# Attention beside an FP4 gated layer: GpSimd out of the gate chain, a finer grid for the pieces, and TensorE's blocks on either side of the values

## The chip, the cores and the metric

The kernel runs on one core of a Trainium2 chip. The metric is the device time in microseconds (us) of one execution: 2633.95 us in the median of 3 runs, 2632.21 to 2635.04. The engines are TensorE (PE; its weight loads are listed as PEld), VectorE (DVE), ScalarE (ACT), GpSimd (POOL) and SyncE (SP, which only issues transfers here).

## The reference

For x of shape (4, 2048, 256) and xn, its layer norm without weights, the result is

```
out = x + attention(xn) + ffn(xn)
attention: q, k, v = split(xn @ Wqkv.T); 16 heads of 16; causal softmax(q k / 4) v; @ Wout.T + bout
ffn:       gate = q4(xn) @ q4(w_gate).T ; up = q4(xn) @ q4(w_up).T      (704 columns)
           h = silu(gate) * up ; y = q4(h) @ q4(w_down).T
q4: blocks of 16 along the last dimension, scale = max|.| / 6, values rounded to the FP4 grid, times scale
```

All is float32.

## The kernel before

Four stages follow one another: the weights, the projections to q, k and v, the largest score of every row (the shift), and the stage that matters here, `main_phase`. It begins shortly before 1000 us and lasts to the end.

In `main_phase` attention and the gated layer run beside each other. Attention is a list of 640 steps. There are 4 batches of 4 groups of 4 heads (`NHG`); a group has 4 chunks of 512 queries, and chunk c has 4(c+1) steps, one for each block of 128 keys at or below the diagonal. So a group has 40 steps. The last four steps of a chunk touch the diagonal and are 512, 384, 256 and 128 queries wide (`Step.width`); all others are 512. In step n TensorE computes the scores of two halves (L1031, and L1037 for the mask) into `S[0]` and `S[1]`, ScalarE makes `probs` of them (L1180, one exp for each half), and TensorE multiplies the probabilities of step n-1 with v into `O` (`values`, L1052). A half of `S` is free for the next scores when its exp is done. When a chunk is over, VectorE turns `O` (L1409, L1410), and only then may the first values of the next chunk write it (semaphore `o_free`); it goes on with sums, reciprocals and scaling (L1414 to L1428; the last, L1428, in every other group). This is `normalise`, and VectorE does it behind all its pieces of that step.

The gated layer handles 64 tiles of 128 tokens, 16 to a batch, 4 to a group of steps. Its work is cut in pieces, and each piece has a place, a mark k out of `MARKS` per tile. `place_marks` spreads the marks of a batch's 16 tiles evenly over the batch's steps, where a step counts as its width plus `STEP_COST`; a mark in the first half of a step is `early`, else `late`. Each engine walks the same list of steps in its own program order, and waits on semaphores where data cross: ScalarE does exp 0, early pieces, exp 1, late pieces; VectorE and GpSimd early, late; TensorE scores, early and late pieces, values of the step before.

The pieces of tile t in order of data, with TensorE's blocks in capitals: X_TURN (L1066) of the quantised x into `F[0]`; ScalarE's `xt_hi` (L1185) and VectorE's `xt_lo` (L1363); GATE for two chunks of 352 columns into `F[0]` and `F[1]`, 6 matmuls each (L1073); VectorE's copy to `gate_sb` (L1368), which frees the bank for UP; GpSimd's `below` = min(gate, 0) (L1255) beside ScalarE's tanh(gate/2) (L1189); ScalarE's `decay` = exp(below) (L1193); GpSimd's gate x decay (L1259); on VectorE the sign bit cleared (L1372), `silu` = (|tanh| + 1) x that (L1376) and `gated` = 0.5 x up x silu (L1380). VectorE then makes the block scales of h (L1331 to L1337), GpSimd normalises (L1244), VectorE rounds (L1341 to L1347), GpSimd scales back (L1250). H_TURN of tile t-1 (L1099) turns it into `F[0]` and `F[1]`, ScalarE makes `ht_hi` (L1198), VectorE `ht_lo` (L1396), and DOWN multiplies in two halves of 9 matmuls into `F[1]` (L1110); VectorE adds it to y (L1402). The same scales, normalising and rounding are done for x, one tile ahead. In half of the tiles two blocks PROJECT (L1119) bring finished attention rows through `Wout`, and VectorE adds them (L1433). SyncE loads x two tiles ahead and stores y at mark 0.

## Time and profile before

| | |
|---|---|
| median of 3 runs | 2633.95 us (2632.21 to 2635.04) |
| profiled execution | 2634.47 us, span 2632.8 us |
| busy, share of the span | PE 2336.7 us (89%), DVE 1962.6 (75%), ACT 1956.8 (74%), POOL 918.4 (35%) |
| mean granted clock of TensorE | 0.975 of full |

The span goes from the first to the last instruction. In the profile a group of instructions has its source line, engine, output and input names without buffer numbers; "idle before" is the time that an engine stood still ahead of an instruction, with what released it. Waits are put down to the last thing that came. Durations overlap on TensorE, as its matmuls are pipelined, so for the length of a block the chain of waits is the better view.

### The profile page before, as it was taken

How to read it: one execution, taken by the hardware profiler on the slowest of the kernel's cores; microseconds unless marked ns; L12 is line 12 of the kernel's file. 1: busy time of each engine (PE TensorE's matmuls, PEld its weight loads, DVE VectorE, ACT ScalarE, POOL GpSimd, SP SyncE). 2: the span in 40 equal slices, each digit the busy share in tenths (PEclk: the TensorE clock that was granted, in tenths of full speed). 3: DMA queues.
4: the chain of work that ended last, by engine and by line, in shares of the span. 5: the costliest groups of instructions: out<-in, count | busy, mean ns of one | idle time of the engine just before them, and what ended most of it. 6: DMA issues, size and time to landing. Idle time of an engine off the chain costs nothing.

```text
span 2632.8 us, 86210 instructions
## 1 busy us (share of the span) xinstructions
PE 2336.7 (89%) x34104; PEld 1294.7 (49%) x34104; DVE 1962.6 (75%) x5676; ACT 1956.8 (74%) x3342; POOL 918.4 (35%) x780
## 2 busy tenths in 40 slices
PE   2896999999999957999999989899998999989998
PEld 1784444444444424445455545455544455554455
DVE  6675999999999975766666667576676666667665
ACT  1343999999999956787777777777777777777775
POOL 3212233333333323333333333333333433334332
PEclk7898999999999988999999999999999999999999
DMA  2576445555555513101201101201011021011000
GB/s 62 176 225 146 69 72 73 73 72 72 73 72 73 72 28 75 28 12 33 61 19 42 38 17 30 60 23 36 22 39 28 13 66 40 19 38 30 13 20 30
DMA packets 94537, 143.82 MB, mean 55 GB/s; under 512 B 24896, under 2 KB 73920, under 8 KB 93632
## 3 DMA queue, kind: packets, MB, share of 16 engines
q1 hardware_dynamic: 89792, 129.50, 25.3%
q0 software_dynamic: 4352, 8.92, 1.4%
q8 instruction: 266, 4.36, 0.7%
q14 instruction: 127, 1.04, 0.2%
HBM read 104.20 MB, written 34.14 MB: 53 GB/s over the span
## 4 chain that ended last, share of the span: by engine, by line
PE 35%; DVE 11%; ACT 10%; issue 7%; DMA 0%; SPq 0%; POOL 0%; DVEq 0%; ACTq 0%; POOLq 0%
PE O L1052 10%; ACT probs L1180 8%; PE F L1073 7%; PE S L1031 6%; PE F L1110 6%; PE F L1119 2%; DVE silu L1376 2%; DVE o_turned L1409 1%; PE S L1037 1%; DVE o_packed L1421 1%; PE F L1099 1%; ACT ht_hi L1198 1%; DVE gated L1380 1%; DVE o_turned L1410 1%; DVE h_amax L1331 1%
## 5 line engine op out<-in xcount | busy, mean ns | idle before, releaser
L1180 ACT ACTIVATE probs<-S 128x1024 f32<-128x1024 f32 (+3 forms) x1280 | 1081.7, 899 | 381.2 <-PE S L1031 195.1
L775 ACT ACTIVATE m_excess<-m_DIFF 128x512 f32<-128x512 f32 (+7 forms) x1536 | 646.8, 472 | 85.0 <-PE m_DIFF L735 39.8
L793 DVE CUSTOM_DVE_ANT_0 m_excess<-m_S,m_excess 128x512 f32<-128x512 f32 (+7 forms) x1536 | 700.5, 530 | 11.1 <-PE m_S L735 9.4
L1052 PE MATMUL O<-probs,v_sb 64*32 64x512 f32 (+3 forms) x10240 | 615.9, 536 | 18.5 <-DVE o_turned L1410 15.8
L1031 PE MATMUL S<-q_st,k_st 64*32 64x512 f16 (+3 forms) x10240 | 440.7, 349 | 141.9 <-ACT probs L1180 99.9
L733 PE MATMUL m_S<-m_k,m_q 128*128 128x512 f16 (+7 forms) x1536 | 482.1, 324 | 26.7 <-DVE m_row_max L793 17.4
L733 PE MATMUL m_DIFF<-m_k,m_q_diff 128*128 128x512 f16 (+7 forms) x1536 | 476.9, 318 | 26.4 <-DMA m_q_diff<-s_q 26.1
L1031 PEld LDWEIGHTS S<-q_st,k_st 64*32 64x32 f16 x10240 | 170.3, 91 | 521.4 <-ACT probs L1180 356.0
L677 POOL TENSOR_TENSOR m_q_diff<-m_zero,m_q 48x4096 f16<-48x4096 f16 x32 | 224.4, 7011 | 428.0 <-DMA m_q<-s_q 417.3
L733 PEld LDWEIGHTS m_S<-m_k,m_q 128*128 128x128 f16 x1536 | 148.0, 96 | 276.7 <-DVE m_row_max L793 195.9
L735 PE MATMUL m_S<-m_future,m_ident 128*128 128x64 bf16 x1024 | 197.0, 193 | 0.0
L735 PE MATMUL m_DIFF<-m_future,m_ident 128*128 128x64 bf16 x1024 | 196.5, 193 | 0.0
L1052 PEld LDWEIGHTS O<-probs,v_sb 64*32 64x32 f32 x10240 | 131.6, 105 | 122.6 <-ACT probs L1180 53.5
L733 PEld LDWEIGHTS m_DIFF<-m_k,m_q_diff 128*128 128x128 f16 x1536 | 150.5, 98 | 69.5 <-issue 27.1
L1376 DVE SCALAR_TENSOR_TENSOR silu<-tanh,gate_sb 128x352 f32<-128x352 f32 x128 | 103.5, 809 | 107.3 <-POOL gate_sb L1259 104.0
L1255 POOL TENSOR_SCALAR below<-gate_sb 128x352 f32<-128x352 f32 x128 | 139.4, 1106 | 91.1 <-DVE gate_sb L1368 90.8
L1227 POOL TENSOR_TENSOR x_norm<-xn,x_rscale 128x256 f32<-128x256 f32 x64 | 39.8, 622 | 366.9 <-DVE x_rscale L1337 366.9
L1250 POOL TENSOR_TENSOR h_fp<-h_norm,h_scale 128x704 f32<-128x704 f32 x64 | 88.9, 1389 | 196.4 <-DVE h_norm L1347 196.4
L1259 POOL TENSOR_TENSOR gate_sb<-gate_sb,decay 128x352 f32<-128x352 f32 x128 | 125.7, 982 | 86.5 <-ACT decay L1193 86.3
L1244 POOL TENSOR_TENSOR h_norm<-gated,h_rscale 128x704 f32<-128x704 f32 x64 | 88.8, 1388 | 182.1 <-DVE h_rscale L1337 182.1
L1368 DVE COPY gate_sb<-F 128x352 f32<-128x352 f32 x128 | 67.1, 524 | 110.0 <-PE F L1073 109.4
L735 PEld LDWEIGHTS m_DIFF<-m_future,m_ident 128*128 128x128 bf16 x1024 | 100.4, 98 | 60.9 <-issue 0.3
(182 smaller groups left out, 4140.8 us busy)
## 6 DMA issues: line engine op xcount, KB each, us to landing
m_q<-s_q SPq DMA_DIRECT2D x96, 128.0 KB, 3.8
m_k<-s_k SPq DMA_DIRECT2D x96, 128.0 KB, 6.8
m_q_diff<-s_q SPq DMA_DIRECT2D x96, 128.0 KB, 8.1
k_st<-s_k SPq DMA_DIRECT2D x96, 128.0 KB, 4.4
q_st<-s_q SPq DMA_DIRECT2D x384, 32.0 KB
m_k<-s_k SPq DMA_DIRECT2D x96, 124.0 KB, 5.3
a_x<-in_L_attn_x_dram POOLq DMA_DIRECT2D x16, 512.0 KB, 4.8
s_q<-a_part SPq DMA_DIRECT2D x32, 256.0 KB, 2.4
```

Source lines behind the costliest of these rows:

```text
L677: pool.tensor_tensor(q_diff[p][rows, :, :], zero[rows, 0:1].unsqueeze(2).to_broadcast([MAX_ROWS, MAX_LOAD, T]), q_st[p][rows, :, :], ALU.s ...
L733: ins = pe.matmul(out[:, 0:keys], q[:, h % MAX_LOAD, i * P:(i + 1) * P], of, start=True, stop=mask is None)
L735: ins = pe.matmul(out[:, keys - PAIR:keys], ident_bf[:, :], mask, start=False, stop=True)
L775: act.activation(excess[u % MAX_EXCESS][:, 0:keys // 2], DIFF[u % MAX_BUFS][:, 0:keys // 2], ACT.Relu) \
L793: dve.tensor_tensor_reduce(larger, S[u % MAX_BUFS][:, 0:keys // 2], larger, 1.0, -3e38, ALU.add, ALU.max, column).then_inc(reduced[u % MAX ...
L1031: ins = pe.matmul(S[half][at, e, 0:st.width], k_st[p][rows, half, st.j * P + at.start:st.j * P + at.stop], q_st[st.chunk % 2][rows, half, ...
L1052: ins = pe.matmul(O[e][s * SLOT:(s + 1) * SLOT, st.skip:QC], v_sb[st.group % 2][rows, st.j, s * SLOT:(s + 1) * SLOT], probs[s // 2][st.n % ...
L1073: ins = pe.matmul(F[ch][:, 0:ICH], m[:, kk * P:(kk + 1) * P], w[:, kk, ch * ICH:(ch + 1) * ICH], start=k == 0, stop=k == len(terms) - 1)
L1110: ins = pe.matmul(F[1][:, 0:D], h[:, m * P:(m + 1) * P], w[:, m, :], start=k == 0, stop=k == len(terms) - 1)
L1180: act.activation(probs[half][st.n % PROBS][:, :, 0:st.width], S[half][:, :, 0:st.width], ACT.Exp, scale=scale).then_inc(exped[half], 1)
L1255: pool.tensor_scalar(below[ch][:, :], gate_sb[ch][:, :], 0.0, None, ALU.min).then_inc(clipped, 1)
L1376: ch.tick(dve.scalar_tensor_tensor(out=silu[c][:, :], in0=tanh[c][:, :], scalar=1.0, in1=gate_sb[c][:, :], op0=ALU.add, op1=ALU.mult))
```

## The change

The grid has 40 marks per tile and a step counts as its width less 85. All places are set anew. TensorE does its late pieces behind the values of the step before, the early ones ahead of them as now. GpSimd's two operations of the gate chain go: `below` is made by VectorE right behind the copy of the gate, and instead of gate x decay VectorE multiplies (|tanh| + 1) with decay, that with the gate and 0.5, and that with up, three products for two. The scratch of the rounding is a buffer for x and one for h.

```diff
--- before.py
+++ after.py
@@ -818,8 +818,8 @@
 
 TILES = T // P
 ALL = B * TILES
-MARKS = 20
-STEP_COST = 110
+MARKS = 40
+STEP_COST = -85
 
 
 def attention_steps():
@@ -850,18 +850,17 @@
             (steps[at].early if due < half else steps[at].late).append((b * TILES + n, k))
 
 
-X_TURN_AT = 4
-GATE_AT, UP_AT = (7, 8), (10, 12)
-H_TURN_AT = 16
-DOWN_AT = (19, 1)
-X_HIGH_AT, TANH_AT, DECAY_AT, H_HIGH_AT = 4, (8, 9), (9, 10), 16
-X_LOW_AT, COPY_AT, GATED_AT, H_LOW_AT, ADD_DOWN_AT = 5, (7, 8), (11, 13), 17, 3
-CLIP_AT, DAMP_AT = (8, 9), (10, 11)
-X_SCALES_AT, X_ROUND_AT, H_SCALES_AT, H_ROUND_AT = 6, 12, 14, 0
-X_NORM_AT, X_RESCALE_AT, H_NORM_AT, H_RESCALE_AT, BIAS_AT, X_LOAD_AT = 7, 14, 17, 4, 13, 0
+X_TURN_AT = 5
+GATE_AT, UP_AT = (9, 16), (13, 20)
+H_TURN_AT = 31
+DOWN_AT = (38, 4)
+X_HIGH_AT, TANH_AT, DECAY_AT, H_HIGH_AT = 5, (19, 20), (14, 19), 33
+X_LOW_AT, COPY_AT, GATED_AT, H_LOW_AT, ADD_DOWN_AT = 8, (9, 17), (18, 29), 34, 7
+X_SCALES_AT, X_ROUND_AT, H_SCALES_AT, H_ROUND_AT = 8, 18, 30, 0
+X_NORM_AT, X_RESCALE_AT, H_NORM_AT, H_RESCALE_AT, BIAS_AT, X_LOAD_AT = 19, 22, 34, 6, 35, 0
 PROJ_FROM, PROJ_TILES = TILES - 3, 8
-PROJ_AT = ((0,), (5,))
-PROJ_ADD_AT = (2, 7)
+PROJ_AT = ((2,), (9,))
+PROJ_ADD_AT = (2, 15)
 HT_SPLIT = 4
 
 
@@ -922,7 +921,7 @@
         xn = sb("xn", [P, D])
         norm = sb("norm", [P, ALL, 2])
         x_scale, x_rscale, x_amax = sb("x_scale", [P, fb]), sb("x_rscale", [P, fb]), sb("x_amax", [P, fb])
-        x_norm, x_fp4, fp4_step = sb("x_norm", [P, D]), sb("x_fp4", [P, D]), sb("fp4_step", [P, I])
+        x_norm, x_fp4, x_step, h_step = sb("x_norm", [P, D]), sb("x_fp4", [P, D]), sb("x_step", [P, D]), sb("h_step", [P, I])
         xt_hi, xt_lo = sb("xt_hi", [P, KD * P], F32R), sb("xt_lo", [P, KD * P], F32R)
         gate_sb, below = two("gate_sb", [P, ICH]), two("below", [P, ICH])
         tanh, decay, silu = two("tanh", [P, ICH]), two("decay", [P, ICH]), two("silu", [P, ICH])
@@ -940,7 +939,7 @@
         x_rs, x_normed, x_rounded, x_ready = sem("x_rs"), sem("x_normed"), sem("x_rounded"), sem("x_ready")
         xt_ps, xt_hi_done, xt_lo_done = sem("xt_ps"), sem("xt_hi_done"), sem("xt_lo_done")
         gate_ps, up_ps, gate_copied, clipped = sem("gate_ps"), sem("up_ps"), sem("gate_copied"), sem("clipped")
-        tanh_made, decayed, damped, gated_done = sem("tanh_made"), sem("decayed"), sem("damped"), sem("gated_done")
+        tanh_made, decayed, gated_done = sem("tanh_made"), sem("decayed"), sem("gated_done")
         h_rs, h_normed, h_rounded, h_ready = sem("h_rs"), sem("h_normed"), sem("h_rounded"), sem("h_ready")
         ht_ps, ht_hi_done, ht_lo_done = sem("ht_ps"), sem("ht_hi_done"), sem("ht_lo_done")
         down_ps, y_added, proj_ps, y_final = sem("down_ps"), sem("y_added"), sem("proj_ps"), sem("y_final")
@@ -1152,10 +1151,12 @@
                     pe.wait_ge(q_ld[st.chunk % 2], 16 * q_dmas * (st.chunk // 2 + 1) + PRIMED)
                 scores(st, 0)
                 scores(st, 1)
-                for t, k in st.early + st.late:
+                for t, k in st.early:
                     pieces(t, k)
                 if st.n:
                     values(steps[st.n - 1])
+                for t, k in st.late:
+                    pieces(t, k)
             values(steps[-1])
             for piece in range(1, len(DOWN_AT)):
                 down(ALL - 2, piece)
@@ -1250,14 +1251,6 @@
                 pool.tensor_tensor(fp4_blocks(h_fp4[:, 0:I]), fp4_blocks(h_norm[:, :]), per_block(h_scale[:, :], hb),
                                    ALU.mult).then_inc(h_ready, 1)
 
-            def clip(t, ch):
-                pool.wait_ge(gate_copied, 2 * t + ch + 1 + PRIMED)
-                pool.tensor_scalar(below[ch][:, :], gate_sb[ch][:, :], 0.0, None, ALU.min).then_inc(clipped, 1)
-
-            def damp(t, ch):
-                pool.wait_ge(decayed, 2 * t + ch + 1 + PRIMED)
-                pool.tensor_tensor(gate_sb[ch][:, :], gate_sb[ch][:, :], decay[ch][:, :], ALU.mult).then_inc(damped, 1)
-
             def place_v(group):
 
                 b, hg = divmod(group, NHG)
@@ -1276,10 +1269,6 @@
                     x_rescale(t + 1)
                 if k == BIAS_AT:
                     add_bias(t)
-                if k in CLIP_AT:
-                    clip(t, CLIP_AT.index(k))
-                if k in DAMP_AT:
-                    damp(t, DAMP_AT.index(k))
                 if k == H_NORM_AT:
                     h_normalise(t)
                 if k == H_RESCALE_AT and t >= 1:
@@ -1317,7 +1306,7 @@
 
         @block.vector
         def _(dve):
-            own = ALL * (2 * (3 + 3) + 2 * 2) + chunks * 4
+            own = ALL * (2 * (3 + 3) + 2 * 3) + chunks * 4
 
             for e in range(2):
                 for p in range(2):
@@ -1356,7 +1345,7 @@
 
             def x_round_(t):
                 dve.wait_ge(x_normed, t + 1 + PRIMED)
-                rounded(x_norm[:, :], fp4_step[:, 0:D], x_rounded)
+                rounded(x_norm[:, :], x_step[:, :], x_rounded)
 
             def x_low(t):
                 dve.wait_ge(xt_hi_done, t + 1 + PRIMED)
@@ -1366,19 +1355,23 @@
             def copy_gate(t, c):
                 dve.wait_ge(gate_ps, 2 * t + c + 1 + PRIMED)
                 dve.tensor_copy(gate_sb[c][:, :], F[c][:, 0:ICH]).then_inc(gate_copied, 1)
+                dve.wait_ge(gate_copied, 2 * t + c + 1 + PRIMED)
+                dve.tensor_scalar(below[c][:, :], gate_sb[c][:, :], 0.0, None, ALU.min).then_inc(clipped, 1)
 
             def gated_chunk(t, c):
                 dve.wait_ge(tanh_made, 2 * t + c + 1 + PRIMED)
                 ch.tick(dve.tensor_scalar(tanh[c][:, :].bitcast(I32), tanh[c][:, :].bitcast(I32), MAGNITUDE, None,
                                           ALU.bitwise_and))
                 ch.sync()
-                dve.wait_ge(damped, 2 * t + c + 1 + PRIMED)
-                ch.tick(dve.scalar_tensor_tensor(out=silu[c][:, :], in0=tanh[c][:, :], scalar=1.0, in1=gate_sb[c][:, :],
+                dve.wait_ge(decayed, 2 * t + c + 1 + PRIMED)
+                ch.tick(dve.scalar_tensor_tensor(out=silu[c][:, :], in0=tanh[c][:, :], scalar=1.0, in1=decay[c][:, :],
                                                  op0=ALU.add, op1=ALU.mult))
                 ch.sync()
+                ch.tick(dve.scalar_tensor_tensor(out=silu[c][:, :], in0=gate_sb[c][:, :], scalar=0.5, in1=silu[c][:, :],
+                                                 op0=ALU.mult, op1=ALU.mult))
+                ch.sync()
                 dve.wait_ge(up_ps, 2 * t + c + 1 + PRIMED)
-                dve.scalar_tensor_tensor(out=gated[t % 2][:, c * ICH:(c + 1) * ICH], in0=F[c][:, 0:ICH], scalar=0.5,
-                                         in1=silu[c][:, :], op0=ALU.mult, op1=ALU.mult) \
+                dve.tensor_tensor(gated[t % 2][:, c * ICH:(c + 1) * ICH], F[c][:, 0:ICH], silu[c][:, :], ALU.mult) \
                     .then_inc(gated_done, 1)
 
             def h_scales(t):
@@ -1388,7 +1381,7 @@
 
             def h_round_(t):
                 dve.wait_ge(h_normed, t + 1 + PRIMED)
-                rounded(h_norm[:, :], fp4_step[:, :], h_rounded)
+                rounded(h_norm[:, :], h_step[:, :], h_rounded)
 
             def h_low(t, part):
                 dve.wait_ge(ht_hi_done, 2 * t + part + 1 + PRIMED)
```

## Rows read from the trace of the kernel before

**Rows 1.** Windows, attention part: us; busy (x) by engine; PEclk, DMA share, GB/s

```profile
1000.00:2600.00 1600.00, 1461.29 (x27620) 805.06 (x27605) 1069.33 (x2232) 1222.96 (x1707) 585.15 (x586) 1.00 0.13 31
```

**Rows 2.** Waits of TensorE, 1000 to 2633 us: total us, times, longest

```profile
PE S L1031 <- ACT probs L1180: 99.0, 278, 0.7
PE O L1052 <- DVE o_turned L1410: 15.8, 15, 1.1
PE F L1110 <- DVE ht_lo L1396: 6.9, 15, 0.5
PE F L1099 <- DVE gated L1380: 5.6, 15, 0.4
PE F L1066 <- DVE y L1433: 3.3, 6, 0.9
```

**Rows 3.** Chain of waits, 1800 to 1880 us: start, us, what

```profile
1802.06 1.06 PE F L1110 x9
...
1834.35 0.37 PE F L1066 x2
...
1835.59 1.02 PE O L1052 x16
1836.60 0.43 PE S L1031 x16
1837.04 2.11 PE F L1073 x12
```

**Rows 4.** Timeline of TensorE: start, us, what; in brackets idle before, releaser

```profile
1805.06 1.09 PE L1052 MATMUL O<-probs,v_sb 64*32 64x512 f32 x16 [1.13 <-DVE o_turned L1410]
...
1816.72 0.41 PE L1031 MATMUL S<-q_st,k_st 64*32 64x512 f16 x8 [0.16 <-ACT probs L1180]
...
1821.58 0.41 PE L1031 MATMUL S<-q_st,k_st 64*32 64x512 f16 x8 [0.45 <-ACT probs L1180]
...
1824.51 0.35 PE L1031 MATMUL S<-q_st,k_st 64*32 64x384 f16 x8 [0.42 <-ACT probs L1180]
...
1833.03 0.41 PE L1031 MATMUL S<-q_st,k_st 64*32 64x512 f16 x8 [0.71 <-ACT probs L1180]
1833.94 0.41 PE L1031 MATMUL S<-q_st,k_st 64*32 64x512 f16 x8 [0.51 <-ACT probs L1180]
```

**Rows 5.** Timeline of ScalarE, 1811 to 1826 us

```profile
1811.02 1.94 ACT L1180 ACTIVATE probs<-S 128x1024 f32<-128x1024 f32 x2 [1.47 <-PE S L1031]
...
1814.88 0.49 ACT L1189 ACTIVATE tanh<-gate_sb 128x352 f32<-128x352 f32 x1
1815.27 0.48 ACT L1193 ACTIVATE decay<-below 128x352 f32<-128x352 f32 x1
...
1822.67 0.87 ACT L1198 ACTIVATE ht_hi<-F 128x512 fp32r<-128x512 f32 x2 [0.22 <-PE F L1099]
```

**Rows 6.** Timeline of VectorE, 1803 to 1836 us, in two normalisations

```profile
1806.24 0.71 DVE L1428 STREAM_TRANSPOSE o_heads<-o_packed 128x512 f32<-128x512 f32 x1
...
1832.43 0.72 DVE L1409 STREAM_TRANSPOSE o_turned<-O 128x512 f32<-128x512 f32 x1 [0.89 <-PE O L1052]
1833.07 0.67 DVE L1410 STREAM_TRANSPOSE o_turned<-O 128x512 f32<-128x512 f32 x1
...
1834.61 0.42 DVE L1421 TENSOR_TENSOR o_packed<-o_sum,o_rsum 128x256 f32<-128x256 f32 x1
```

**Rows 7.** Groups by line and shape, 1200 to 2600 us: busy, mean ns

```profile
L1255 POOL TENSOR_SCALAR below<-gate_sb 128x352 f32<-128x352 f32 x112 | 121.9, 1106 | 84.1 <-DVE gate_sb L1368 83.9
...
L1259 POOL TENSOR_TENSOR gate_sb<-gate_sb,decay 128x352 f32<-128x352 f32 x110 | 108.0, 982 | 74.2 <-ACT decay L1193 73.9
...
L1376 DVE SCALAR_TENSOR_TENSOR silu<-tanh,gate_sb 128x352 f32<-128x352 f32 x110 | 89.2, 811 | 90.7 <-POOL gate_sb L1259 87.8
...
L1380 DVE SCALAR_TENSOR_TENSOR gated<-F,silu 128x352 f32<-128x352 f32 x110 | 57.7, 524 | 3.8
...
L1372 DVE TENSOR_SCALAR tanh<-tanh 128x352 int32<-128x352 int32 x111 | 44.9, 404 | 0.0
```

## The prediction

> **What bounds the kernel now.** I read the profile page first, then the busy times by windows. The attention and gated layer fill 1000 to 2600 us; there TensorE is busy 1461.29 of 1600 us, ScalarE 1222.96, VectorE 1069.33, GpSimd 585.15, and the granted clock is 1.00 [rows 1]. So 138.7 us of TensorE idle time is the most that a new order can take out of this part. The waits of TensorE name nearly all of it: 99.0 us for an exp of ScalarE before the next scores, 15.8 us for VectorE to empty O, 6.9 us for `ht_lo`, 5.6 us for the gated product, 3.3 us before the turn of x [rows 2]. The change does not touch the stages before 1000 us.
>
> The chain of waits prices the blocks [rows 3]: scores of a full step 0.43 us, values 1.02, two gate products 2.11 (one 1.06), half a down product 1.06, the turn of x 0.37; a projection has as many columns as half a down product, and I count it as 1.06. A full step without a block needs 0.43+1.02 = 1.45 us of TensorE, but two exps, 1.94 us, of ScalarE. With one block it needs 2.51 and ScalarE falls behind only if it gets over 0.5 us of its own pieces. So lost time sits in steps with nothing, or little, on TensorE and much on ScalarE. The places are seen in the timeline [rows 4]: within one group of 40 steps (4 tiles; 16 groups fill this part), TensorE waits 0.45 us after an empty step, 0.42 after the turns of h, 0.71+0.51 around the empty step 12, 0.16 around the up products, and 1.13 for VectorE in step 1. I number steps 0 to 39 in a group; chunks end at steps 3, 11, 23 and 39, and each batch repeats the same 40 places four times.
>
> **The grid.** Every piece is placed by counting width+110 per step, now width-85. By the code a group has 40 steps, 17408 of width, and 80 marks (160 after), so 272.6 per mark of 20 before, 87.55 per mark of 40 after. A full step holds 2.28 of 20 marks before, 4.88 of 40 (2.44 of 20) after; a 128-wide step 0.87 before, 0.49 (0.25) after. I went through the 40 steps of both plans. Before: both gates in steps 4, 14, 24 and 33, an up product in each of the two steps behind; after: gate 0 in 2, 13, 22, 31, then up 0, gate 1, up 1 in one step each. Empty or nearly empty full steps before: 7, 12, 17, 27, 32, 36; after: 7, 17, 27, 35.
>
> **Part 1, values in front of late blocks.** At each chunk's end VectorE turns O (0.72+0.67 us [rows 6]) and the next chunk's first values wait for it. At step 0 the last values of the old chunk stood behind a projection and a half down product (1.06+1.06). After the change they stand in front; between them and the next values lie both blocks, the scores of step 1 and the turn of x, some 3 us, against 1.39 us of VectorE. Where no projection is there, still 1.06+0.43+0.4 = 1.9 us cover it. VectorE's add of the projection comes ahead of its turning in program order and eats 0.4+1.06 us of that cover in projecting tiles: 2.9 needed, 3.0 there. So 15.8 us go, and with them the 3.3 us before the turn of x, whose add no longer stands behind the whole normalisation: -19 us. Bounds: 0 (the cover just missed) and -19.1. Late now: nothing at step 1, but see part 4.
>
> **Part 2, empty steps.** Step 12 gets the down half and the turn of x, so its 0.71+0.51 us [rows 4] go: 1.22 x 16 groups = -19.5 us. In exchange gate 0 is in step 13 and needs `xt_lo`, which VectorE makes behind the normalisation of chunk 1 (2.6 us from 1832.43 to its end, 0.71 more where heads are turned [rows 6]), the add of the down product and itself (as `o_packed`, 256 values, 0.42 each). From the start of step 12: values end at 0.81, VectorE is through at 4.3 or 5.0, TensorE wants gate 0 at 3.7: a new wait of 0.6 or 1.3; in projecting tiles TensorE has a projection more on both sides and the wait is 0 to 0.2. Mean 0.5 x 16 = 8 us. Net -11; bounds +2 and -19.5. The four empties that stay cost the same as now.
>
> **Part 3, ScalarE's pieces.** The high part of h moves from between a step's two exps to behind both (early 16 of 20, now late 33 of 40). Before, ScalarE waited 0.22 us for the turns and took 0.87 for the two copies ahead of the second exp [rows 5], and TensorE paid 0.42 [rows 4]; the turns stand early in all four tiles, the fourth in a 384-wide step whose exps are shorter, for which I take 0.27: 1.53 x 16 = 24.5 us. After, the copies delay only the next step's exps, which have a down half to hide behind. But `ht_lo` is then made later: after the turns TensorE has values, scores, values (2.5 us) until the down half; ScalarE and VectorE need about 2.5 to 2.9 us. I give back 0.1 to 0.4 us in three tiles. Take -14; bounds 0 and -24.5. Around the products, tanh and decay take 0.39 each behind an exp [rows 5]; before, three of the four fell in one step (1.94+1.17 = 3.1 against 2.5 of TensorE), after it is two (2.7 against 2.5), then one. The wait there is 0.16 us [rows 4], four times a group some 0.2, 13 us: take -6, bounds -13 and +19 (in steps 5 and 25 `decay` waits for a clip that VectorE now makes behind the normalisation, up to 0.6 us twice a group).
>
> **Part 4, GpSimd's two operations go to VectorE.** GpSimd loses 128 x (1106+982 ns) = 267 us [rows 7], none of it on TensorE's path. VectorE gains a clip, not in the trace before; nearest is the AND over the same 128x352 values, one input and a constant too, 404 ns; above it lies `gated` with 524. I take 404. Per chunk before (the copy is in both): AND 404, silu 811, gated 524, sum 1739 ns. After: clip 404, AND 404, and three products at 524, as `gated` has it; `silu`, with as many values, is slower only while GpSimd works beside it, I assume, and half of that work goes. Sum 2380, so +0.64 us x 128 = 82 us busy. Bounds: all three products at 811 give +1.5 us per chunk, clip and AND at half of `gated` +0.36. VectorE stands at 67% in this part, so busy time is hidden; what is not hidden is the tight stretch behind a normalisation. Before, h's scales, rounding and `ht_lo` just met TensorE: the 6.9+5.6 us of [rows 2] are one wait of each per group. 1.3 us more per tile in front of them, less the 1.06 us of gate 0 that moves out of TensorE's stretch too, makes these waits longer. I take +10 us, bounds -12.5 (both waits gone) and +35 (another 0.5 us per tile). The rounding scratch split in two (`x_step`, `h_step`) removes no wait, as one engine uses both in order: 0. The latency from copy to gated falls (GpSimd's 1.11 and 0.98 us against 0.40 and 0.52) and pays only where `silu` waited.
>
> The Trainium skill speaks against this part: "VectorE: DVE Perf Modes", section Rules for kernel authors, says to minimise the number of chained VectorE operations, since each flushes its pipeline whatever the semaphores. By the rows the count costs busy time on an engine that is busy 1069.33 of 1600 us, and the price of an operation is in its duration; by the rule taken alone the added 82 us would bear on the end and outweigh the gains, which is the slower rival below.
>
> GpSimd's pieces that remain (normalise, rescale, bias) depend on VectorE as before and now queue behind nothing of the gate chain. SyncE's loads and stores keep their place at mark 0; a tile's load waits for the bias, which sits at 35 of 40 against 13 of 20, i.e. later by 4.5 marks of 20 and two tiles ahead of use: nothing. The end of the kernel behind the last step keeps its order: 0, give or take 1.
>
> **Sum.** -19 -11 -14 -6 +10 = -40 us. From the profiled execution's 2634.5 us (span 2632.8 and 1.7 around it; 0.5 above the median of 2633.95) this is 2594; I round up for the waits at the copies and forecast **2596 us**. Own range of this case 2577 to 2614.
>
> **Rivals.**
> (a) The waits only move: part 2's and 3's gains are given back as waits for `xt_lo`, `ht_lo` and gated; parts 1 and 4 stay, -19+10: 2625, 2615 to 2634. For it: VectorE already meets TensorE with 0.4 us short; against: three of the four empty-step places have no chunk end.
> (b) VectorE's delays all stay hidden, only the four empty steps (about 31 us), the 256-wide steps and the like remain: -19-19.5-24.5-13 = -76: 2558, from 2550 to 2577. For it: VectorE 67%; against: the stretch behind a normalisation.
> (c) Slower: VectorE becomes the engine that TensorE waits for behind each chunk end. The place is steps 0 to 9 and 12 to 14: `xt_lo` and the gate copies stand behind 2.6 to 3.3 us of normalisation, with 1.3 us more per tile. Price: 1.3 at step 13, 0.5 at step 2 and at 22, 0.6 at 5 and 25, 0.4 for each `ht_lo` and each gated in four tiles, 6.7 us per group, 107 us, against 76 of gains and 12.5 of old such waits that it contains: +19, 2653. It decides from 5.5 us a group on.
> (d) TensorE's time within the blocks grows or nothing of the ScalarE waits goes (they are a property of exp's latency, not of the order): within 5 us, 2634.
>
> **Chances.** Forecast 0.50, (a) 0.18, (b) 0.12, (c) 0.14, (d) 0.06. A measurement here can tell 0.2%, 5.3 us. All of the forecast and of (b), and 0.14 of (a), are faster: 0.76, less 0.02 for errors in hidden terms: 0.74. Same: 0.04 of (a), 0.05 of (d), 0.01 of (c): 0.10. Slower: 0.16. The range 2562 to 2638 leaves out most of (c) and the far end of (b).
>
> **What would show it.** In 1000 to about 2570 us: scores waiting for exp fall from 99 us to about 60; the O wait falls from 15.8 to under 3; waits for `ht_lo` and gated rise from 12.5 to 20 or more; a new row, the gate product waiting for `xt_lo`, near 8 us; `silu` near 524 ns; GpSimd's busy time about 651 us, VectorE's about 2045. The forecast is wrong if waits of TensorE for VectorE rise by over 50 us, if the exp waits stay above 90, or if TensorE's busy time in this part is not 1461 plus or minus 10.

## The result and the profile after

The changed kernel takes 2539.59 us (median of 4 runs, 2538.29 to 2541.21) against 2633.08 (2632.12 to 2635.04): ratio 0.9644, 95% interval 0.9628 to 0.9661, or 93.5 us less. The forecast was 38 less, and the time lies below the range. The profiled execution took 2539.19 us, its span is 2537.5, so 95.3 us went from the span. Up to 1000 us both kernels have the same picture (TensorE busy 848.34 us, 849.33 before).

Page of the changed kernel, the busy times; before, the same line had TensorE 2336.7, weight loads 1294.7, VectorE 1962.6, ScalarE 1956.8 and GpSimd 918.4:

```profile
PE 2314.7 (91%) x34104; PEld 1273.9 (50%) x34104; DVE 2038.4 (80%) x5932; ACT 1952.0 (77%) x3342; POOL 645.4 (25%) x524
```

VectorE and GpSimd came out near the forecast (2045 and 651). TensorE has the same 34104 matmuls and 22.0 us less busy time, which the forecast had at nothing; 21.1 of it lies behind 1000 us. Windows view from there to the end, before and then after:

```profile
1000.00:2632.80 1632.80, 1487.41 (x27968) 823.66 (x27952) 1086.89 (x2267) 1233.47 (x1724) 590.73 (x591) 1.00 0.13 31
```

```profile
1000.00:2537.50 1537.50, 1466.36 (x27968) 803.57 (x27968) 1162.09 (x2522) 1229.49 (x1725) 317.80 (x334) 1.00 0.14 33
```

Windows view, the counterpart of [rows 1] up to 2500 us; TensorE is idle for 64.5 of 1500 us, where it was idle for 138.7 of 1600:

```profile
1000.00:2500.00 1500.00, 1435.50 (x27558) 782.59 (x27558) 1142.67 (x2482) 1214.07 (x1702) 314.33 (x331) 1.00 0.14 33
```

Waits of TensorE from 1000 us to the end, for [rows 2] (engine, tile, line <- what it waited for: us in total, times, longest):

```profile
PE S L1030 <- ACT probs L1181: 42.9, 119, 0.5
PE F L1072 <- DVE xt_lo L1352: 9.8, 18, 1.3
PE F L1065 <- POOL x_fp L1234: 5.5, 1, 5.5
PE F L1118 <- DVE y L1395: 4.4, 7, 1.0
PE F L1098 <- DVE y L1395: 2.6, 1, 2.6
PE O L1051 <- ACT probs L1181: 1.0, 2, 0.8
```

Three rows of [rows 2] are gone: the emptying of O (15.8 us), `ht_lo` (6.9) and gated (5.6). The waits for an exp fell from 99.0 us in 278 waits to 42.9 in 119. The sum over TensorE, from the two profiles:

| term | measured | forecast |
|---|---|---|
| waits for an exp | 99.0 to 42.9, -56.1 | about -50 (19.5 + 24.5 + 6) |
| O emptied | -15.8 | -15.8 |
| waits for `ht_lo` and gated | 12.5 to 0, -12.5 | +20.5 (10.5 given back + 10) |
| gate 0 waits for `xt_lo` | +9.8 | +8 |
| y (3.3 at the turn of x, now 4.4 at L1118) | +1.1 | -3.3 |
| start of the part and other single waits | +1.6 | 0 |
| TensorE's busy time | -22.0 | 0 |
| sum | -93.9 (span: -95.3) | -40.6, in the prediction -40 |

Timeline of TensorE in the changed kernel, 1698 to 1703 us, around the turns of h (L1098) and the down half that needs `ht_hi` and `ht_lo` (L1109):

```profile
1698.18 0.41 PE L1030 MATMUL S<-q_st,k_st 64*32 64x512 f16 x8
1699.09 0.41 PE L1030 MATMUL S<-q_st,k_st 64*32 64x512 f16 x8 [0.51 <-ACT probs L1181]
1699.43 0.87 PE L1098 MATMUL F<-ident,h_fp 128*128 128x128 f32 x6
1700.24 1.09 PE L1051 MATMUL O<-probs,v_sb 64*32 64x512 f32 x16
1701.12 0.64 PE L1030 MATMUL S<-q_st,k_st 64*32 64x512 f16 x16
1701.55 1.06 PE L1051 MATMUL O<-probs,v_sb 64*32 64x512 f32 x16
1702.55 0.38 PE L1109 MATMUL F<-w_down_hi,ht_hi 128*128 128x256 f32 x1
```

And ScalarE and VectorE of the same kernel in the same stretch:

```profile
1700.73 0.91 ACT L1199 ACTIVATE ht_hi<-F 128x512 fp32r<-128x512 f32 x2
1701.49 0.96 DVE L1389 TENSOR_TENSOR ht_lo<-F,ht_hi 128x512 fp32r<-128x512 f32 x2
```

Two things are to be seen. The turns end at 1700.30 and `ht_lo` at 1702.45: 2.15 us, where I had taken 2.5 to 2.9, and the down half starts at 1702.55 without a wait, with 0.10 us to spare. And scores that wait between their halves are two entries of 0.41 us, 0.82 of busy time, while scores without a wait are one entry of 16 matmuls and 0.64.

Groups of VectorE in the changed kernel, 1200 to 2500 us (busy, mean ns), for [rows 7]:

```profile
L1367 DVE SCALAR_TENSOR_TENSOR silu<-tanh,decay 128x352 f32<-128x352 f32 x109 | 73.5, 674 | 3.8
...
L1374 DVE TENSOR_TENSOR gated<-F,silu 128x352 f32<-128x352 f32 x110 | 57.7, 524 | 3.8
L1330 DVE TENSOR_SCALAR h_step<-h_norm 128x704 int32<-128x704 int32 x55 | 57.5, 1045 | 34.6 <-POOL h_norm L1245 34.6
L1370 DVE SCALAR_TENSOR_TENSOR silu<-gate_sb,silu 128x352 f32<-128x352 f32 x109 | 57.2, 525 | 3.7
...
L1359 DVE TENSOR_SCALAR below<-gate_sb 128x352 f32<-128x352 f32 x109 | 39.5, 362 | 3.8
...
L1363 DVE TENSOR_SCALAR tanh<-tanh 128x352 int32<-128x352 int32 x109 | 36.4, 334 | 0.0
```

Clip, AND and three products are 362 + 334 + 674 + 525 + 524 = 2419 ns a chunk; I had 2380.

### The profile page after: what moved, and what is told of

It reads as the page before. It is cut to its first block, busy times and chain, and to the rows that moved or that the text cites. A ratio compares the mean times of both kernels' runs of the same rounds, so it can differ in the third digit from the quotient of the medians.

```text
span 2537.5 us, 86209 instructions
## 1 busy us (share of the span) xinstructions
PE 2314.7 (91%) x34104; PEld 1273.9 (50%) x34104; DVE 2038.4 (80%) x5932; ACT 1952.0 (77%) x3342; POOL 645.4 (25%) x524
## 3 DMA queue, kind: packets, MB, share of 16 engines
q1 hardware_dynamic: 89792, 129.50, 26.1%
## 4 chain that ended last, share of the span: by engine, by line
PE 47%; ACT 7%; issue 5%; DVE 3%; DMA 0%; SPq 0%; POOL 0%; DVEq 0%; ACTq 0%; POOLq 0%
PE O L1051 16%; PE F L1072 10%; PE S L1030 9%; ACT probs L1181 6%; PE F L1109 5%; PE F L1118 2%; PE F L1098 2%; PE S L1036 1%; DVE o_turned L1402 0%; ACT xt_hi L1186 0%; DVE o_turned L1403 0%; PE S L1118 0%; DMA v_in<-s_v 0%; DVE o_sum L1407 0%; DVE xt_lo L1352 0%
## 5 line engine op out<-in xcount | busy, mean ns | idle before, releaser
L733 PE MATMUL m_S<-m_k,m_q 128*128 128x512 f16 (+7 forms) x1536 | 482.6, 324 | 26.7 <-DVE m_row_max L793 17.4
L1030 PE MATMUL S<-q_st,k_st 64*32 64x512 f16 (+3 forms) x10240 | 414.9, 350 | 82.7 <-ACT probs L1181 43.8
L1030 PEld LDWEIGHTS S<-q_st,k_st 64*32 64x32 f16 x10240 | 148.9, 90 | 412.7 <-ACT probs L1181 251.4
L1051 PEld LDWEIGHTS O<-probs,v_sb 64*32 64x32 f32 x10240 | 148.0, 105 | 69.9 <-ACT probs L1181 32.1
L1234 POOL TENSOR_TENSOR x_fp<-x_norm,x_scale 128x256 f32<-128x256 f32 x64 | 41.8, 652 | 442.0 <-DVE x_norm L1336 442.0
L1109 PE MATMUL F<-w_down_hi,ht_hi 128*128 128x256 f32 x384 | 122.7, 319 | 0.0
L1036 PE MATMUL S<-future,quarter 64*32 64x32 bf16 (+3 forms) x4096 | 119.6, 197 | 0.0
L1072 PE MATMUL F<-w_gate_hi,xt_hi 128*128 128x352 f32 x256 | 98.6, 385 | 9.8 <-DVE xt_lo L1352 9.8
```

What stands on the lines that cost most here:

```text
L733: ins = pe.matmul(out[:, 0:keys], q[:, h % MAX_LOAD, i * P:(i + 1) * P], of, start=True, stop=mask is None)
L1030: ins = pe.matmul(S[half][at, e, 0:st.width], k_st[p][rows, half, st.j * P + at.start:st.j * P + at.stop], q_st[st.chunk % 2][rows, half, ...
L1036: ins = pe.matmul(S[half][at, e, 0:at.stop], quarter[rows, :], future[rows, P - at.stop:P], start=False, stop=True)
L1051: ins = pe.matmul(O[e][s * SLOT:(s + 1) * SLOT, st.skip:QC], v_sb[st.group % 2][rows, st.j, s * SLOT:(s + 1) * SLOT], probs[s // 2][st.n % ...
L1072: ins = pe.matmul(F[ch][:, 0:ICH], m[:, kk * P:(kk + 1) * P], w[:, kk, ch * ICH:(ch + 1) * ICH], start=k == 0, stop=k == len(terms) - 1)
L1109: ins = pe.matmul(F[1][:, 0:D], h[:, m * P:(m + 1) * P], w[:, m, :], start=k == 0, stop=k == len(terms) - 1)
```

## The experiments

The change has three parts that can be made alone: **G**, GpSimd's two operations to VectorE (and the split scratch); **O**, TensorE's late blocks behind the values; **P**, the grid, the step cost and all places. The expectations of the first runs had P alone bring most of the gain and O alone its 15.8 us; the other possibility is that the parts work only together. All eight combinations, medians in us, with the waits of TensorE from 1000 us on ("busy" is TensorE's in the whole span):

| | time | ratio (95%) | exp | O emptied | `xt_lo` | `ht_lo` + gated | busy |
|---|---|---|---|---|---|---|---|
| before | 2633.6 | 1 | 99.0 | 15.8 | - | 12.5 | 2336.7 |
| G (g_only) | 2638.09 | 1.0017 (1.0007-1.0027) | 93.2 | 26.1 | - | 17.4 | 2333.3 |
| P (p_only) | 2785.77 | 1.0575 (1.0557-1.0593) | 90.4 | 10.1 | 51.1 | 62.3 | 2370.0 |
| O (o_only) | 2650.76 | 1.0067 (1.005-1.0083) | 102.8 | 43.2 | - | - | 2336.5 |
| P+O (no_g) | 2616.55 | 0.994 (0.9924-0.9957) | 83.6 | 1.5 | 9.8 | 24.7 | 2327.2 |
| G+O (no_p) | 2668.11 | 1.0136 (1.0119-1.0153) | 102.5 | 54.7 | - | - | 2340.0 |
| G+P (no_o) | 2708.1 | 1.0282 (1.0265-1.0299) | 54.7 | 10.2 | 50.7 | 36.6 | 2354.8 |
| all (after) | 2539.6 | 0.9644 (0.9628-0.9661) | 42.9 | - | 9.8 | - | 2314.7 |

**g_only**, before with G alone:

```diff
+                dve.tensor_scalar(below[c][:, :], gate_sb[c][:, :], 0.0, None, ALU.min).then_inc(clipped, 1)
...
-CLIP_AT, DAMP_AT = (8, 9), (10, 11)
```

> The kernel before with GpSimd's two operations given to VectorE and nothing else (20 marks, cost 110, TensorE's old order). Theory P (the places do it: the gain is in exp waits that the plan avoids): 2628 to 2645, exp waits of TensorE near 99 us as before. Rival G (the gate chain was late everywhere; GpSimd out of it makes ht_lo and gated meet TensorE): the waits for ht_lo and gated, 12.5 us, vanish and the exp waits fall too: 2590 to 2615.

Measured 4.5 us more, within theory P's range: exp waits fall by 5.8 us, the O wait rises by 10.3 and `ht_lo` with gated by 4.9. Of my +10 for the waits in front of h, the old places show 4.9.

**p_only**, before with all of P's constants, of which the first two are shown (GpSimd's product is written over `decay` and read from there, as tanh now comes behind decay):

```diff
-MARKS = 20
-STEP_COST = 110
+MARKS = 40
+STEP_COST = -85
...
```

> The kernel before with the new grid, cost and places alone; GpSimd keeps clip (marks 10 and 18) and the product (15 and 20), which it now writes over decay, since tanh is placed behind decay. Theory P: 2565 to 2590, exp waits about 45 to 60 us. Rival G (the new places need the short chain): 2600 to 2640, with waits for gated and ht_lo of over 30 us.

152 us slower, outside both ranges expected. Waits of TensorE in it:

```profile
PE S L1031 <- ACT probs L1180: 90.4, 194, 0.9
PE F L1073 <- DVE xt_lo L1363: 51.1, 34, 3.7
PE F L1110 <- DVE ht_lo L1396: 37.8, 47, 0.8
PE F L1099 <- DVE gated L1380: 24.5, 62, 0.4
PE F L1119 <- DVE y L1402: 24.4, 10, 3.4
```

The new places alone make TensorE wait for VectorE's data at four of its blocks. Part of the loss is the clock: TensorE's busy time is 33.3 us longer, with a granted clock of 0.98 between 1000 and 2500 us against 1.00 before.

**o_only**, before with O alone:

```diff
-                for t, k in st.early + st.late:
+                for t, k in st.early:
                     pieces(t, k)
                 if st.n:
                     values(steps[st.n - 1])
+                for t, k in st.late:
+                    pieces(t, k)
```

> The kernel before with TensorE's late blocks behind the values and nothing else. Theory O (values in front free O early, and fewer stalls): the 15.8 us of waits for o_turned go, 2612 to 2620. Rival: the old places put two gates late in one step, so that values in front only shift the wait: 2628 to 2636.

17 us slower, outside both ranges expected. `ht_lo` and gated go, as in the changed kernel, but the wait for O grows to 43.2 us, with the old places.

**no_g**, the changed kernel without G (GpSimd's clip at marks 10 and 18, its product at 15 and 20):

```diff
+CLIP_AT, DAMP_AT = (10, 18), (15, 20)
```

> The changed kernel with clip and product back on GpSimd (marks 10 and 18, 15 and 20; the product is written over decay). Theory (chain behind the chunk end: VectorE's and GpSimd's work from the last values to the products of a tile sets the time where the places are close): the two GpSimd operations lengthen that path, 2570 to 2620, waits for gated and ht_lo of 20 us or more. Rival (with the new order the path has slack, and GpSimd out of it is worth as little as it was alone): 2535 to 2550.

It lies 77 us above the changed kernel, within the range of the theory, with exp waits of 83.6 us against 42.9: at these places half of the gain in exp waits needs G. ScalarE's waits in it hold one for `below`, GpSimd's clip; in the changed kernel ScalarE waits for `below` once, 0.7 us:

```profile
ACT decay L1195 <- POOL below L1257: 60.2, 64, 1.5
```

**no_p**, before with the diffs of g_only and o_only:

> The changed kernel with the old grid, cost and places; order and VectorE's work are the new ones. Theory (the order pays only by letting the places close up): near the order alone, 2645 to 2665, exp waits about 100 us. Rival (order and GpSimd out of the chain suffice together): 2560 to 2610.

It came 3 us above the range of the theory, with the exp waits that it named.

**no_o**, the changed kernel with `for t, k in st.early + st.late` in front of the values:

> The changed kernel with TensorE's old order (all blocks in front of the values). If the order is worth its 15.8 us of o_turned waits alone: 2553 to 2560. If the new places lean on it (late blocks wait for data that came in time before): 2575 to 2600 with longer waits for xt_lo, y or gated. If it is worth nothing: 2538 to 2545.

G+P has nearly the exp waits of the changed kernel (54.7 against 42.9) but 50.7, 36.6 and 24.0 us for `xt_lo`, `ht_lo` and y. So O is worth -168.5 us with G and P and +17 alone; P is worth -128.5 with G and O and +152 alone; G is worth -77 with P and O and +4.5 alone. No part is a gain by itself: the parts don't add up, they work together. The size of no_o's loss was missed (2575 to 2600 expected), and part of it, too, is a granted clock of 0.98.

**cost110**, the changed kernel with the old cost of a step on the new grid:

```diff
-STEP_COST = -85
+STEP_COST = 110
```

> The changed kernel with STEP_COST 110 for -85, so narrow steps take more marks and full ones fewer, all places as numbers unchanged. Theory (what counts is that pieces leave the narrow steps, where a chunk ends and ScalarE is short of work, for the full ones): 2560 to 2600, more exp waits. Rival (the numbers of the places count, the weight of a step hardly): 2535 to 2552.

2665.88 us, 1.0122 (1.0105-1.0139), 126 us over the changed kernel. Exp waits are 105.3 us, `gate_sb` 28.9, `xt_lo` 26.1. Worked out from `place_marks`, both tanh, one decay and up 1 then fall into one full step in three of four tiles, gate 1 and up 0 with the other decay into the step before it, and TensorE has nothing in seven full steps of a group, where it has nothing in four now. The loss is nearly that of undoing all of P (128.5 us), and larger than either expectation. As the places were chosen for the new cost, this does not price cost and places apart.

**hh_early**, part 3 of the prediction undone:

```diff
-X_HIGH_AT, TANH_AT, DECAY_AT, H_HIGH_AT = 5, (19, 20), (14, 19), 33
+X_HIGH_AT, TANH_AT, DECAY_AT, H_HIGH_AT = 5, (19, 20), (14, 19), 31
```

> The changed kernel with H_HIGH_AT at 31 for 33: ScalarE copies the high part of h between the two exps of the step, as before the change, in most tiles. By part 3 of the prediction the second exp comes 0.75 to 1.1 us later and TensorE pays 0.3 to 0.42 us in each of 64 tiles: exp waits +20 to +27 us, 2555 to 2567. Rival (ht_lo in time is worth the same, or the exps hide it): 2535 to 2545.

2569.45 us, 0.976 (0.9743-0.9776), 2 us above the theory's range: 30 us more, 0.47 a tile. The exp waits are 63.6 us in 166 (+20.7, 47 more waits) and the busy time 2323.3 (+8.6), 0.18 us per added wait. Part 3's gross price of 24.5 us lies between the 20.7 us of waits and the 30 of time, and nothing of it was given back.

**o_norm** (before with O, VectorE normalises ahead of its late pieces) and **norm_first** (the changed kernel with the same), to see whether VectorE's order costs the O wait and the `xt_lo` wait:

```diff
-                for t, k in st.late:
-                    pieces(t, k)
...
+                for t, k in st.late:
+                    pieces(t, k)
```

> The kernel before with TensorE's new order, and VectorE's normalise in front of its late pieces of the step instead of behind them. Theory (the order alone was slower because VectorE's late gate copies, in steps 4 and 24, now wait for gates behind the values and hold up normalise): the 43.2 us of waits for o_turned of the order alone fall under 5, and 2650.8 becomes 2600 to 2620. Rival (the order alone is slow for another reason, such as ScalarE or a switch of blocks): 2640 to 2655.

> The changed kernel with VectorE's normalise in front of its late pieces. With the new places hardly a VectorE piece that waits stands late in a chunk-end step (only adds of projections), so by the theory the change is small: 2532 to 2546. Rival (the adds in front of normalise still cost): 2515 to 2530, with the 9.8 us of waits for xt_lo halved.

Both came out slower than expected. In o_norm the O wait of 43.2 us went, as expected, but the time rose to 2691.35 (1.0217, 1.02-1.0234): exp waits 130.0 us, and gate products wait 31.6 us for the add of a projection, which now stands behind the normalisation. norm_first took 2570.47 (0.9757, 0.974-0.9773), with waits for that add of 20.4 and 5.0 us, and `xt_lo` at 9.4 as before it. The O wait of o_only is thus a matter of VectorE's order, but the late pieces have deadlines too.

**o_ends**: values in front of late blocks only in the step behind a chunk's end. If the order pays only where O is emptied, as part 1 had it, this is as fast as the changed kernel.

```diff
-                for t, k in st.early:
+                ends = st.n and steps[st.n - 1].last
+                for t, k in st.early + ([] if ends else st.late):
```

> The changed kernel, but TensorE does late blocks behind the values only in the first step of a chunk (16 of the 160 steps of a batch); elsewhere all blocks stand in front. Theory (the order counts because VectorE's normalisation starts with the last values of a chunk): 2536 to 2556, no waits for ht_lo. Rival (the order is needed in all steps, since late pieces of ScalarE and VectorE feed late blocks): 2580 to 2700, with waits for ht_lo and xt_lo as without the order.

2612.04 us, 0.9917 (0.9902-0.9932): 72 us over, in the rival's range. TensorE in it:

```profile
1710.41 0.89 PE L1098 MATMUL F<-ident,h_fp 128*128 128x128 f32 x6
1711.23 1.09 PE L1051 MATMUL O<-probs,v_sb 64*32 64x512 f32 x16
1712.11 0.37 PE L1030 MATMUL S<-q_st,k_st 64*32 64x384 f16 x8
...
1713.56 0.39 PE L1109 MATMUL F<-w_down_hi,ht_hi 128*128 128x256 f32 x1 [0.81 <-DVE ht_lo L1390]
```

Its waits:

```profile
PE S L1030 <- ACT probs L1182: 40.9, 105, 0.5
PE F L1109 <- DVE ht_lo L1390: 35.1, 47, 0.8
PE F L1072 <- DVE xt_lo L1353: 31.8, 29, 2.3
PE F L1118 <- DVE y L1396: 11.6, 10, 1.8
```

From the turns of h to the down half there is one block of values, not two, and TensorE stands 0.81 us for `ht_lo`; the same between the turn of x and gate 0. In every step, not at chunk ends alone, the order gives a late block's inputs the 1.02 us of a step's values [rows 3] more.

**no_g_placed**: GpSimd keeps its two operations, with places of their own for them (tanh 14 and 19, decay 19 and 22, product 20 and 23, gated 22 and 29). Were no_g's loss only a matter of places, this would come near the changed kernel; the rival was GpSimd's latency wherever it stands.

```diff
-X_HIGH_AT, TANH_AT, DECAY_AT, H_HIGH_AT = 5, (19, 20), (14, 19), 33
+X_HIGH_AT, TANH_AT, DECAY_AT, H_HIGH_AT = 5, (14, 19), (19, 22), 33
-X_LOW_AT, COPY_AT, GATED_AT, H_LOW_AT, ADD_DOWN_AT = 8, (9, 17), (18, 29), 34, 7
+X_LOW_AT, COPY_AT, GATED_AT, H_LOW_AT, ADD_DOWN_AT = 8, (9, 17), (22, 29), 34, 7
...
+CLIP_AT, DAMP_AT = (10, 18), (20, 23)
```

> GpSimd in the chain as in no_g, with tanh ahead of decay again and decay, product and gated later (tanh 14 and 19, decay 19 and 22, product 20 and 23, gated 22 and 29). Theory (ScalarE's 56 us of waits for GpSimd's clip, which hold up exps, are the main loss): they fall under 10, time 2565 to 2595; the waits for gated, 25 us, stay or grow. Rival (GpSimd's two microseconds in the chain are the loss wherever decay stands): 2605 to 2630.

2644.22 us, 1.0041 (1.0028-1.0054), above both ranges expected. ScalarE no longer waits for the clip and the exp waits are those of the changed kernel, but the turns of h wait for gated:

```profile
PE F L1099 <- DVE gated L1382: 55.7, 77, 1.1
PE S L1031 <- ACT probs L1182: 41.7, 116, 0.5
```

At these places the wait only moves from ScalarE's queue to the end of the chain. TensorE's busy time is 2356.1 us, 41.4 over the changed kernel's, and a good part of that is not GpSimd's latency but the clock. Windows view, 1000 to 2500 us (granted clock 0.98; no_g has 1.00), then the turns of h and what follows them, and the window of 4 us there:

```profile
1000.00:2500.00 1500.00, 1381.35 (x25800) 739.21 (x25801) 1023.28 (x2090) 1145.43 (x1595) 544.58 (x548) 0.98 0.13 32
```

```profile
1091.29 0.63 PE L1099 MATMUL F<-ident,h_fp 128*128 128x128 f32 x4
1092.75 0.45 PE L1099 MATMUL F<-ident,h_fp 128*128 128x128 f32 x2 [0.83 <-DVE gated L1382]
1093.13 1.96 PE L1052 MATMUL O<-probs,v_sb 64*32 64x512 f32 x16
```

```profile
1093.00:1097.00 4.00, 4.00 (x77) 1.64 (x80) 3.27 (x7) 1.83 (x4) 2.08 (x2) 0.57 0.02 6
```

Behind the wait for gated the granted clock falls to 0.57 and a block of values takes 1.96 us, 1.09 elsewhere. Over 1500 us 0.98 makes some 30 us, an estimate. So the rival (GpSimd's latency costs wherever decay stands) is borne out by the 55.7 us for gated, for the one set of places tried, and its range is not.

**fill_p0, fill_norm**: one of the two projections goes from mark 2 to 26, into an empty step, still in `F[0]` (the waits for the bank change with it); fill_norm has norm_first's order too.

```diff
-PROJ_AT = ((2,), (9,))
-PROJ_ADD_AT = (2, 15)
+PROJ_AT = ((9,), (26,))
+PROJ_ADD_AT = (15, 27)
```

> The changed kernel with one of the two projections of a tile, which stands at mark 2 with a down half beside it, moved to mark 26 into the empty step behind up 1 (bank F[0], its add at 27; the other projection stands at 9 as before and uses F[1] as before). Theory (an empty full step and the exp wait behind it cost 0.45 to 0.5 us, and two blocks in one step are surplus): 32 tiles x 0.5 + the drain of as many waits, 15 to 25 us less, 2514 to 2525, exp waits 43 to about 28. Rival (the work only changes place, TensorE is the bound): 2535 to 2545.

> Both edits, the projection in the empty step and normalise in front of the late pieces: the sum of the two if they are independent, 2505 to 2530; not under the better of the two if the first already removes what the second would.

fill_p0 took 2556.58 us (0.9704, 0.9687-0.972), fill_norm 2581.6 (0.9801, 0.9785-0.9817), both slower than the changed kernel and than expected. In fill_p0 the exp waits fell by 13.6 us to 29.3 in 87, as expected, but the projection is ahead of the data: gated is waited for at two places, 13.7 and 9.5 us, and TensorE's busy time is 10.8 us longer.

**fill_late** has the projection at mark 28 and its add at 30, **fill_add** the add at 29. **after_again** is the changed kernel again, on the same chip as fill_late_again and fill_add.

> The projection in the empty step once more, now late in it (mark 28) with its add at 30, ahead of h's scales: the product's bank is free by then. Theory (VectorE's latency was what ate the gain, 13.7 us of waits for gated before the projection and 9.5 before the turns of h): these fall under 8 together, exp waits near 30 us, 2512 to 2532. Rival (the add of the projection in the tight stretch of VectorE costs as much as the exp waits gained): 2536 to 2556.

> As fill_late_again with the projection's add at mark 29, ahead of gated on VectorE, for 30. If the waits of the turns of h are VectorE's queue: they go and the time falls to 2524 to 2530. Rival (VectorE now stands waiting for the projection and gated comes late): the waits for y turn into waits for gated of as much or more, 2534 to 2545.

> The changed kernel unaltered, beside the next two on one chip: 2538 to 2542.

> The projection late in the empty step (mark 28, add at 30) once more, on the chip of the run above: 2533 to 2537, 3 to 6 us under it. Rival (the 4 us were the chips' difference): within 2 us of it.

fill_late took 2535.44 us (0.9627, 0.9614-0.964), and again 2534.6 (2531.89 to 2535.79; 0.9625, 0.9612-0.9638) beside 2539.51 (2537.35 to 2541.3; 0.9643, 0.963-0.9656) of the changed kernel: 4.9 us, with ranges of times that don't meet, though the intervals of the two ratios overlap. It is the fastest version measured, though fill_late lies between its two expected ranges and not in the theory's. Of the 13.5 us of exp waits that it saves, 9.3 come back as the turns of h waiting for the add of the projection. fill_add took 2562.57 (0.973, 0.9717-0.9744), above both ranges expected. Its waits:

```profile
PE F L1098 <- DVE gated L1374: 16.9, 14, 1.2
PE F L1098 <- ACT probs L1181: 15.5, 13, 1.2
```

One mark earlier, VectorE stands for the projection (its waits for L1118 are 41.6 us in 27, 20.8 in 13 in the changed kernel) with everything else queued behind it, and 28 us are lost against fill_late_again to save 9.2. The second row names an exp, but in the code the turns of h wait for `h_fp`, gated and the add alone, so that wait was most likely for VectorE too.

## Why the prediction was wrong

- **Part 4 and the give-back of part 3 failed; they are 33 of the 56 us between the forecast and the time.** The time lies below every range that I gave, that of (b) too. I let `ht_lo` and gated wait 20.5 us longer; both waits are gone. The step that failed is "After, the copies delay only the next step's exps ... But `ht_lo` is then made later: ... need about 2.5 to 2.9 us". The trace has 2.15 us against 2.25 of TensorE's blocks. The +10 of part 4 was priced against the old order: g_only shows +4.9 us of it there, o_ends 35.1 for `ht_lo` with the new places without the order, and the changed kernel nothing. I had weighed part O at the chunk ends alone ("Part 1, values in front of late blocks"), and o_ends shows that this left out most of it: 72 us. By no_o (`ht_lo` 36.6 us, gated 0) and no_g (gated 24.7, `ht_lo` 0) it is the order that hides `ht_lo` at the new places, and part 4 that hides gated.
- **Part 4 was priced as a cost (+10 us), "none of it on TensorE's path", and is worth 77 us in the plan.** ScalarE's `decay` waits for GpSimd's clip for 60.2 us in no_g, ahead of exps that TensorE needs: 40.7 of its 83.6 us of exp waits are gone without GpSimd. no_g_placed has the small exp waits with GpSimd in the chain, and pays 55.7 us for gated instead.
- **TensorE's busy time, taken as fixed, fell by 22.0 us.** A pair of score halves split by a wait is 0.82 us busy, one unsplit 0.64. There are 159 fewer exp waits: 159 x 0.18 = 29, an estimate from these two rows, against 22 measured; hh_early gives 8.6 us for 47 waits, the same 0.18. But no_g has 80 exp waits and 62 for gated more than the changed kernel and only 12.5 us more busy time, 0.09 a wait, and fill_late 32 exp waits fewer, 26 for the add more, and the same busy time. So in the pairs in which only the number of waits grew, a wait cost 0.09 to 0.18 us beyond its own length. Some 2 us of the 22 are the clock: before, TensorE stood once for 2.88 us at 1700 us, and the granted clock of the 7 us around it is 0.68 (7 x 0.32, an estimate). The sign that I had set, 1461 plus or minus 10 us of busy time in this part, was badly set, as it leaves out the end: from 1000 us to the end it is 1466.36 us, where it was 1487.41 before. And the 138.7 us of idle time were no upper bound on the gain, as the busy time could fall too. The window of before:

```profile
1700.00:1707.00 7.00, 4.12 (x20) 3.43 (x12) 0.80 (x3) 2.54 (x3) 1.28 (x2) 0.68 0.57 173
```

- **Part 1** was right in size for O (-15.8), in part by luck. With the new places and without the order 10.2 us of the wait are left (no_o), so the places took 5.6, and with the old places the order makes the wait longer (43.2). The 1.06 us of a projection is right, but its reason is not: a projection has 4 matmuls of 256 columns, half a down product 9. The y row did not go but moved to L1118, +1.1 for the -3.3 forecast.
- **Part 2**: the new wait is 9.8 us in 18, forecast 8, and exp waits fell by 56.1 against some 50 for parts 2, 3 and the products together. hh_early gives part 3 alone as 30 us, of them 20.7 in waits. How the rest divides between the empty step and the products was not tried.
- **The rivals**: (b), 2558, all VectorE delays hidden, was nearest. It took TensorE's busy time as fixed like the rest, and 22 below it is 2536. (c), VectorE behind chunk ends, is what no_o shows: the price was real, 50.7 us for `xt_lo`, and the order takes it away. (a) and (d) are out.
- **The indicators**: the exp waits (42.9, said 60), those for `ht_lo` and gated (0, said 20 or more) and `silu`'s first product (674 ns, said 524) came out off, the O wait, `xt_lo`, GpSimd and VectorE as said.
- The rule that speaks for fewer VectorE operations, from the Trainium skill, "VectorE: DVE Perf Modes", section Rules for kernel authors, did not decide here: two operations a chunk more (256 in all, +75.8 us busy) go with 77 us less (no_g). By the waits of no_g and no_g_placed the latency of the chain weighs more than the count.

What stays open: why the wait for O is 43.2 us in o_only and 54.7 in no_p yet absent with P was only followed in the order (o_norm takes it away), not block by block. And how much of each kernel's loss is the clock and how much the waits themselves was not separated; the sums of waits alone leave it out.

## What to carry to other kernels

Order, places and the engine of a chain of work are one plan: tried one at a time, each part of this one loses (+4.5, +17 and +152 us), and together they save 94, so test a part inside the plan that it belongs to, and by taking it out too. Price a wait against the blocks between producer and consumer, with latencies read from a timeline, and count the block of values that a new order puts between them in every step. In an in-order queue leave a piece behind the others until its input is there: VectorE standing early (28 us) cost more than TensorE waiting for it (9.2 us). And look at the granted clock where waits grow: what they cost can be more than their length.

## What the runs showed of the hardware

- Scores that wait between their halves cost 0.82 us of TensorE's busy time and 0.64 without the wait. From 332 waits of TensorE before to 149 after (all kinds, from 1000 us on), its busy time in this part fell by 21.1 us, some 2 of them by the clock.
- VectorE's AND over 128x704 takes 1045 ns (527 before) in the kernel in which GpSimd's bias add runs beside it. The places decide it, not who does the gate chain: with the old places it is 525 to 527 ns in all five kernels (g_only, o_only, no_p and o_norm too), with the new ones 1034 to 1046 (cost110, with the old cost of a step: 903). Timeline of GpSimd, then VectorE, in the changed kernel:

```profile
1703.00 0.75 POOL L1241 TENSOR_TENSOR y<-x_in,bias 128x256 f32<-128x256 f32 x1
```

```profile
1703.08 1.05 DVE L1330 TENSOR_SCALAR h_step<-h_norm 128x704 int32<-128x704 int32 x1 [0.64 <-POOL h_norm L1245]
1704.16 0.53 DVE L1332 TENSOR_SCALAR h_step<-h_step 128x704 f32<-128x704 f32 x1
```

  The next operation over as many values, with GpSimd quiet, takes 0.53 us. The AND over 128x352 takes 334 ns, 404 before, when GpSimd was busy nearly twice as long.
- `silu`'s first product takes 0.83 us at 1460.28, where GpSimd's `x_fp` (0.65 us from 1460.08) runs beside it, and 0.53 at 1462.51, where GpSimd is quiet, both in the changed kernel; the mean is 674 ns.
- The granted clock between 1000 and 2500 us is 0.98 in p_only, no_o, o_norm and no_g_placed, 0.99 in o_ends, cost110, no_p, norm_first and fill_norm, and 1.00 in the changed kernel. In the first two TensorE stood for up to 3.7 us at a time; in no_g_placed the longest waits that come back are those of 1.1 us in the turns of h, and behind one of 0.83 us the granted clock was 0.57 in the next 4 us, so for most of them at the lower of the two levels, 1.2 GHz; values took 1.96 us there for 1.09.
